# Leftover keys scored and applied in eight single pieces in the middle of each attention sweep

## The reference, cut to what matters

```python
x = x + jnp.tanh(g_xattn[3]) * _L3_xattn_ref(...)      # q, k, v projections, then per head:
# scores = q @ k.T * 8 ** -0.5 ; p = softmax(scores, axis=-1) ; out = (p @ v) @ Wo + bo
x = x + jnp.tanh(g_ffn[3]) * _L3_ffn_ref(_layernorm(x, axis=-1), ...)
```

## Time and profile before

| | us |
|---|---|
| median of 3 runs | 3082.24 (3079.79 to 3084.54) |
| the profiled execution, its time | 3080.51 |
| its span on the core | 3078.7 |
| TensorE (PE) busy | 3009.3, 98% |
| ScalarE (ACT) busy | 2519.7, 82% |
| VectorE (DVE) busy | 467.2, 15% |
| exponentials of the sweeps, x2496 | 2283.0 |
| value products (line 2343) | 1324.3 |
| score products (line 2362) | 1064.4 |
| chain that ended last | PE 94% |

### The profile page before, as it was taken

How to read it: one execution, slowest core, us unless ns; L and a number is a source line. 1 busy time by engine, 2 the same in 40 slices (tenths; PEclk the granted TensorE clock), 3 DMA queues, 4 the chain that set the end, 5 groups by cost and what they waited for, 6 DMA issues and landing times.

```text
span 3078.7 us, 54520 instructions
## 1 busy us (share of the span) xinstructions
PE 3009.3 (98%) x18701; PEld 1140.2 (37%) x18701; DVE 467.2 (15%) x1308; ACT 2519.7 (82%) x2893; POOL 206.1 (7%) x732
## 2 busy tenths in 40 slices
PE   7999999999999899999999998999999999999999
PEld 5333333323334433333323334666522222332257
DVE  4200001001011400111101004544200000000012
ACT  3899999999933499999999995322499999999963
POOL 4000000000000000000000002000000000000000
PEclk9999999999999999999999999999999999999999
DMA  7122122112220112122211223110011111111110
GB/s 198 54 63 64 58 63 68 38 37 63 63 75 0 29 58 69 54 63 65 64 38 39 63 63 112 32 37 1 8 38 37 37 37 54 47 38 36 37 38 8
DMA packets 167028, 157.27 MB, mean 51 GB/s; under 512 B 20872, under 2 KB 121724, under 8 KB 166844
## 3 DMA queue, kind: packets, MB, share of 16 engines
q1 hardware_dynamic: 159872, 149.27, 16.1%
q0 software_dynamic: 1088, 3.34, 0.3%
q10 hardware_dynamic: 5884, 2.08, 0.3%
HBM read 121.89 MB, written 32.91 MB: 50 GB/s over the span
## 4 chain that ended last, share of the span: by engine, by line
PE 94%; DVE 3%; DMA 1%; issue 1%; ACT 1%; SPq 1%; ACTq 0%; DVEq 0%
PE PS L2343 40%; PE PS L2362 31%; PE PS L774 5%; PE PS L759 5%; PE PS L761 2%; PE PS L1114 2%; PE PS L1104 1%; PE PS L1572 1%; PE PS L1569 1%; PE PS L1148 0%; PE PS L1105 0%; PE PS L2323 0%; PE PS L2253 0%; PE PS L2329 0%; PE PS L1134 0%
## 5 line engine op out<-in xcount | busy, mean ns | idle before, releaser
L2110 ACT ACTIVATE probs<-PS 128x1024 f32<-128x1024 f32 x2496 | 2283.0, 1227 | 37.8 <-PE PS L2362 32.9
L2343 PE MATMUL PS<-probs,vr 128*32 128x512 f32 (+1 forms) x9984 | 1324.3, 603 | 1.9 <-DVE accs L2590 1.9
L2362 PE MATMUL PS<-qs,kr 35*128 35x512 f32 (+2 forms) x4992 | 1064.4, 481 | 8.7 <-ACT probs L2110 3.3
L2362 PEld LDWEIGHTS PS<-qs,kr 35*128 35x128 f32 x4992 | 448.0, 184 | 1181.9 <-ACT probs L2110 816.0
L797 ACT ACTIVATE probs<-PS 128x512 f32<-128x512 f32 x192 | 114.5, 598 | 273.6 <-PE PS L759 145.5
L1939 POOL COPY vr<-vs 128x72 f32 (+1 forms) x624 | 157.8, 253 | 2668.9 <-PE PS L2343 2466.5
L2343 PEld LDWEIGHTS PS<-probs,vr 128*32 128x32 f32 x9984 | 197.2, 108 | 339.2 <-issue 272.1
L774 PEld LDWEIGHTS PS<-wide,probs 128*128 128x128 f32 x1280 | 152.7, 195 | 17.5 <-issue 16.5
L774 PE MATMUL PS<-wide,probs 128*128 128x128 f32 x1280 | 155.1, 279 | 0.5 <-DVE kf L832 0.5
L2590 DVE COPY accs<-PS 128x512 f32<-128x512 f32 x12 | 8.3, 692 | 750.1 <-PE PS L2329 750.1
L759 PE MATMUL PS<-xT,wide 128*128 128x512 f32 x224 | 106.7, 594 | 1.0 <-DVE probs L816 1.0
(11 more groups left out here) (315 smaller groups left out, 1185.8 us busy)
## 6 DMA issues: line engine op xcount, KB each, us to landing
kr<-key_pieces SPq DMA_DIRECT2D x1248, 64.0 KB
key_pieces<-kparts SPq DMA_DIRECT2D x172, 96.0 KB, 2.8
kr<-mask_strips SPq DMA_DIRECT2D x624, 4.0 KB
values<-kf SPq DMA_DIRECT2D x34, 216.0 KB, 4.2
vs<-values SPq DMA_DIRECT2D x2, 3672.0 KB, 16.1
c_T<-turned_context SPq DMA_DIRECT2D x18, 192.0 KB, 4.0
key_pieces<-probs SPq DMA_DIRECT2D x32, 96.0 KB, 2.9
c_in<-turned_context SPq DMA_DIRECT2D x16, 192.0 KB, 4.3
```

The source lines that it names most:

```text
L2110: sc.activation(prob[n % RING][:, :, q0:], PS[:, bank:bank + 2, q0:], ACT.Exp, scale=SCALE).then_inc(p_ready, 1)
L2343: last = te.matmul(PS[32 * j:32 * j + 32, 7, q0:], vr[s.buf(c)][:, at_v:at_v + 32], prob[(n + j // 2) % RING][:, j % 2, q0:], start=fresh, ...
L2362: last = te.matmul(o, kr[b][own, p, :], qs[own, T8 // 2 * s.hh + p, 512 * s.qh + q0:512 * s.qh + 512], start=True, stop=True)
```

## The change

The leftover keys are now handled inside the sweep that they belong to. Round 9 (`LEFT_ROUND`) takes the four score products one at a time and round 10 takes the value product in four pieces of 128 columns. Each piece stands behind a value group, in four neighbouring half chunks: behind (c, g) = (0, 1), (1, 0), (1, 1) and (2, 0). The exponential stands in ScalarE's list between rounds 9 and 10. The seams and the ends of the attentions have only the last value groups left. VectorE's copy of the accumulator waits for the last value group (`pv_done`) as well. The items of round 9 are moved to the third chunk of round 10, those of round 10 to the first of round 11, those of round 11 behind them. The loops of sweeps 8, 9 and 11 on TensorE are cut in two, with six chunks written out between them.

```diff
@@ ScalarE
                         for p in range(4):
                             exps(c, p)
-                            if prev and (c, p) == (0, 1):
-                                exps_left(prev)
                     with act.Fori(1, EXP_ROUND) as i:
...
                                 exps(c, p, i)
+                    exps_left(s)
...
-                    if s.w % NSW == NSW - 1:
-                        exps_left(s)
@@ TensorE
+                def left_free(s):
                     if s.w % NSW == 0:
                         pe.wait_ge(left_in, LEFT_IN * (a + 1))
                     if s.w:
                         pe.wait_ge(left_done, s.w)
+                    if s.w % NSW == 2:
+                        if a == 0:
+                            pe.wait_ge(early_ev, EARLY_AT[0] + 3)
+                        else:
+                            pe.wait_ge(r_cen, (0, 1, 3)[a])
+                    own = [(w, i) for w in range(s.w + 1) for i in range(1, ROUNDS_S) if w < s.w or i < LEFT_ROUND]
+                    pe.wait_ge(v_ev, NTILE + sum(len(later_items(w, i)) for w, i in own))
+                def left_score(s, tt):
+                    if tt == 0:
+                        left_free(s)
+                    t8 = T8 // 2 * s.hh + tt
+                    last = te.matmul(PS[:, 6, :], k_left[:, P * t8:P * t8 + P], qs[:, t8, 512 * s.qh:512 * s.qh + 512], start=(tt == 0), stop=(tt == T8 // 2 - 1),
+                                     skip_group_check=True)
+                    if tt == T8 // 2 - 1:
+                        last.then_inc(left_ready, 1)
+                def left_value(s, k):
+                    if k == 0:
+                        pe.wait_ge(left_done, s.w + 1)
+                    last = te.matmul(PS[:, 7, k * P:k * P + P], v_left[:, s.hh, :], p_left[:, k * P:k * P + P], start=False, stop=True, skip_group_check=True)
+                    if k == 3:
+                        last.then_inc(left_used, 1)
+                def left_slot(s, i, c, g):
+                    slot = 2 * c + g - 1
+                    if i == LEFT_ROUND and 0 <= slot < 4:
+                        left_score(s, slot)
+                    if i == LEFT_ROUND + 1 and 0 <= slot < 4:
+                        left_value(s, slot)
...
                         values(prev, prev.n - 1, 0)
-                        left_scores(prev)
                     scores(0, 1)
                     if prev:
                         values(prev, prev.n - 1, 1)
-                        left_values(prev)
...
                             items = later_items(s.w, i)
+                            if i == LEFT_ROUND:
+                                items = []
+                            if i == LEFT_ROUND + 1:
+                                items = [None] * (TC - 1) + later_items(s.w, LEFT_ROUND)
+                            if i == LEFT_ROUND + 2:
+                                items = later_items(s.w, i - 1) + items
...
                                     values(s, i * TC + c - 1, g)
+                                    left_slot(s, i, c, g)
...
-                        with pe.Fori(1, ROUNDS_S) as i:
+                        with pe.Fori(1, LEFT_ROUND) as i:
...
+                        for c in range(LEFT_ROUND * TC, (LEFT_ROUND + 2) * TC):
+                            for g in range(2):
+                                scores(c, g)
+                                values(s, c - 1, g)
+                                left_slot(s, c // TC, c % TC, g)
+                        with pe.Fori(LEFT_ROUND + 2, ROUNDS_S) as i:
@@ VectorE
                     dve.wait_ge(left_used, s.w + 1)
+                    dve.wait_ge(pv_done, s.quads + 2 * s.n)
```

More of the change, by code:

```diff
@@ L57 @@
 EXP_ROUND = 10
+LEFT_ROUND = EXP_ROUND - 1
 NSW = 4
@@ L1171, in early_dve @@
                 dve.wait_ge(left_ready, 2)
+                dve.wait_ge(pv_done, SWEEPS[2].quads)
                 leaf_turn_dve(dve, 0, 6).then_inc(early_ev, 1)
@@ L1784, in _ @@
                                 sp.wait_ge(left_ready, s.w)
+                                sp.wait_ge(pv_done, s.quads)
                             if 2 * TC <= c < 2 * TC + 6 and a == 0:
@@ L2312, in _ @@
                 pe.wait_ge(qc_dve, QU // 2 * (a + 1))
-                def left_scores(s):
+                def left_free(s):
                     if s.w % NSW == 0:
@@ L2319, in left_scores @@
                         pe.wait_ge(left_done, s.w)
-                    pe.wait_ge(v_ev, NTILE + sum(len(later_items(w, i)) for w in range(s.w + 1) for i in range(1, ROUNDS_S)))
-                    for tt in range(T8 // 2):
-                        t8 = T8 // 2 * s.hh + tt
-                        last = te.matmul(PS[:, 6, :], k_left[:, P * t8:P * t8 + P], qs[:, t8, 512 * s.qh:512 * s.qh + 512], start=(tt == 0), stop=(tt == T8 // 2 - 1))
-                    last.then_inc(left_ready, 1)
-                def left_values(s):
-                    pe.wait_ge(left_done, s.w + 1)
-                    te.matmul(PS[:, 7, :], v_left[:, s.hh, :], p_left[:, :], start=False, stop=True, skip_group_check=True).then_inc(left_used, 1)
+                    if s.w % NSW == 2:
[25 more added lines that the diff above has]
+                        left_value(s, slot)
                 def values(s, c, g, i=0):
@@ L2383, in _ @@
                                     values(s, i * TC + c - 1, g)
-                                if c < len(items):
+                                    left_slot(s, i, c, g)
+                                if c < len(items) and items[c]:
                                     later_pe(pe, *items[c])
@@ L2388, in _ @@
                     else:
-                        with pe.Fori(1, ROUNDS_S) as i:
+                        with pe.Fori(1, LEFT_ROUND) as i:
+                            for c in range(TC):
+                                for g in range(2):
+                                    scores(c, g, i)
+                                    values(s, c - 1, g, i)
+                        for c in range(LEFT_ROUND * TC, (LEFT_ROUND + 2) * TC):
+                            for g in range(2):
+                                scores(c, g)
+                                values(s, c - 1, g)
+                                left_slot(s, c // TC, c % TC, g)
+                        with pe.Fori(LEFT_ROUND + 2, ROUNDS_S) as i:
                             for c in range(TC):
@@ L2398, in _ @@
                     if s.w % NSW == NSW - 1:
-                        left_scores(s)
                         for g in range(2):
                             values(s, s.n - 1, g)
-                        left_values(s)
                 between_pe(pe, a)
```

## The result

| | before | after |
|---|---|---|
| median | 3081.01 (3078.21 to 3084.54, 4 runs) | 3136.65 (3121.90 to 3150.18, 4 runs) |
| ratio, 95% interval | | 1.0172 [1.0145, 1.0198] |
| the profiled execution, its time | 3080.51 | 3150.18 |
| its span | 3078.7 | 3148.4 |

A later comparison of the same two kernels gave 3134.93 us and 1.0181 [1.0143, 1.0219] (the last experiment). The forecast was 3104.0 us, 3088 to 3111. The direction was right and the size was not: of 55.6 us, it had 22.5. Executions of one kernel differ by up to 28 us here (3121.90 to 3150.18), and the profiled one of after is its slowest; the fastest had a mean granted clock of TensorE of 0.984, the slowest of 0.973.

The account below looks back on a forecast made before the run. ScalarE sets the pace, TensorE waiting 0.17 us a half chunk. Gains of 11.9 us against costs of 34.4 give net 22.5 us more: 3103.0 from the profiled execution, 3104.7 from its median; forecast 3104.0 us, range 3088 to 3111.

Parts of the forecast that it names:

- part 5: First sweep of each attention: the first score piece waits for operand loads; 15.0 us lost, 13.5 to 19.2.
- estimate of 12.6 us: Loss from the three operand waits by the skill page's fixed DMA cost of about 2.0 us: 12.6 us.
- The slack of 0.17 us a half: Steady half chunk: it repeats every 1.83 us, TensorE needs 1.66, so its lag shrinks by 0.17 us.
- Rival C: At the operand waits: loads land in time or the wait is met earlier; 15.0 us go, 3090 us; chance 0.09.
- Rival E: Late key loads, loop switching beyond the cushion, or operands landing at 4.2 us: 3109 to 3112 us; chance 0.06.
- B: Rounds 9 and 10: pieces are seamless and cost their columns alone; net +5.4 us, 3088 us; chance 0.08.
- D: Mid sweep: the cushion is deeper, up to 2.75 us, so pieces lose nothing; +1.1 us, 3083 us; chance 0.05.
- part 3: Rounds 9 and 10: lone pieces take 0.43 and 0.41 us, losing 1.26 us a sweep, 15.1 us; exponentials 1.5 us.
- part 4: Items moved behind the pieces in six sweeps: 2.6 us lost, and 0.2 us for transposes in sweep 2.
- parts 1 and 2: Leftover work gone from the seams gains 6.0 and 0.5 us, from the three attention ends 5.4 us.
- what would show it wrong: Halves with a piece last no longer than those without, or the first piece starts unwaited in the first sweeps.
- the cushion: TensorE's lead over ScalarE: inserted work is hidden up to 0.54 us, everything above is ScalarE's loss.

Follow-up runs that it names:

- the last experiment: The changed kernel run once more, unchanged, against the kernel before: 3134.93 us, ratio 1.0181.
- the filled wait: The changed kernel with 25, 25 and 18 unused products ahead of the operand wait in sweeps 0, 4 and 8: 3116.63 us, ratio 1.0119.
- the first experiment: The changed kernel with two small v_left loads per chunk instead of one, all landed long before round 9: 3093.19 us, ratio 1.0033.
- The two lumps: The first experiment with four score products together in round 9 and the value product whole in round 10: 3088.91 us, ratio 1.0027.
- The waits without pieces: The changed kernel without the leftover keys' products and exponentials, but with the operand wait in sweeps 0, 4 and 8: 3099.37 us, ratio 1.0058.

## Why the prediction was wrong

**The step that failed is part 5, the price of the wait.** It said that all of the wait is ScalarE's loss, and stopped there: 15.0 us, 19.2 at most. Its length was nearly right: 5.84, 6.20 and 4.62 us of standstill against 5.65, 5.56 and 3.83, because the load let TensorE go 3.07, 3.51 and 3.66 us after its issue and not after 2.8 (2374.82 - 2371.16 in sweep 8). The prediction's estimate of 12.6 us was further off: the Trainium skill, DMA: Bandwidth & Descriptors, Anatomy of one DMA, gives its fixed cost of about 2.0 us for the path of GpSimd, and this load is SyncE's. What was missing is that TensorE's speed depends on TensorE not standing still. The slack of 0.17 us a half, by which the whole sum is made, exists at 2.4 GHz only; at 1.2 GHz TensorE needs 3.01 us for a half that ScalarE needs 1.83 for, and each such half loses 1.18 us, or 3.74 - 1.83 = 1.91 with a piece. Over 20 to 34 us of low clock this comes to 29.2 us for the three in the first trace and 23.7 in the second, against 17.0 for the length of the waits. The sum had this term at nothing. Put into it: 3104.7 + 1.6 for the longer waits + 29.2 is 3135.5, and with 23.7 it is 3130.0; the medians were 3136.65 and 3134.93. That the first of the two comes so near is partly luck, since its 29.2 is from the slowest execution.

The profile of before could have warned me. It has stretches of low clock in the opening of sweep 0 (10.2 us from 99.7) and between the attentions, and I read the clock only where I wanted to know the pace. The Trainium skill, TensorE: Matmul & The Clock Gate, HAM oscillation — how this bites in real kernels, tells of a kernel whose waits for DMAs let the clock fall each time. The traces agree: it fell behind each of the fourteen unfilled waits of 2.27 us and more. I did not weigh it. It prices the fall as half of the throttled time. By that, as an estimate, the 75.1 us of low clock at the three places in the first trace would be 37.5; the comparison with the filled wait gives 29.2, since part of the low clock lies in the standstill and in what ScalarE's own pace covers.

**Rival C was the kernel one edit away.** It had 3090 for no wait; the early loads gave 3093.19. Its mechanism, that the loads land in time, was wrong for the changed kernel and its price was good. Rival E named later operands and gave 3109 to 3112; it had the right side and the wrong mechanism. B and D fell: the pieces are neither seamless nor hidden.

**Right, the pieces (part 3).** In sweep 9, which no wait disturbs:

```profile
2568.11 0.49 PE L2333 MATMUL PS<-qs,k_left 128*128 128x512 f32 x1
...
2570.20 0.49 PE L2333 MATMUL PS<-qs,k_left 128*128 128x512 f32 x1
...
2576.45 0.73 PE L2385 MATMUL PS<-qs,kr 35*128 35x512 f32 x4
2577.11 1.06 PE L2366 MATMUL PS<-probs,vr 128*32 128x512 f32 x8
2578.11 0.49 PE L2385 MATMUL PS<-qs,kr 35*128 35x512 f32 x2
...
2580.29 0.49 PE L2342 MATMUL PS<-p_left,v_left 128*128 128x128 f32 x2
...
2582.37 0.49 PE L2342 MATMUL PS<-p_left,v_left 128*128 128x128 f32 x2
```

A half with a score piece takes 2.09 us and one with a value piece 2.08, against 2578.11 - 2576.45 = 1.66: 0.43 and 0.42 us a piece, where 0.43 and 0.41 were forecast. A value piece has a quarter of a score piece's columns, in two passes, and costs as much; about half of each is the fixed part. The two lumps take 1.13 + 1.05 us of TensorE in place of 4 x 0.43 + 4 x 0.42 = 3.4, and the 1.2 us saved are six times 0.2. With the Trainium skill's rule, TensorEngine Tiling (Array Packing), Key Properties, that a change of tiling mode drains TensorE, the runs agree; they show the price of a product that stands alone, and not that the drain is what it pays for. Rival B's price, the columns alone, would have made the pieces free to ScalarE, and they were not. ScalarE lost 1.22 to 1.30 us a sweep in sweeps 1, 3, 5, 7, 8, 9 and 11 of the first experiment; 1.26 was the forecast.

**Right, the items (part 4).** From before to the first experiment, rounds 9 to 11 lose 17.8 us more over the twelve sweeps. Parts 3 and 4 have 15.1 + 2.6 + 0.2 = 17.9.

**Right, the seams and the ends (parts 1 and 2).** ScalarE runs through the seam from sweep 8 to 9, where the earlier trace rows have an idle time of 0.72 us, and in the second attention the next work starts close behind the last exponential:

```profile
2464.15 13.57 ACT L2113 ACTIVATE probs<-PS 128x1024 f32<-128x1024 f32 x14
```

```profile
1936.50 0.71 ACT L2113 ACTIVATE probs<-PS 128x256 f32<-128x256 f32 x2 [0.31 <-DVE PS L2624]
```

```profile
1937.26 0.43 PE L2366 MATMUL PS<-probs,vr 128*32 128x128 f32 x8 [0.23 <-ACT probs L2113]
1937.62 3.70 PE L760 MATMUL PS<-h_T,wide 128*128 128x512 f32 x8
```

From the last exponential's end, 1937.21, to the next product there are 0.41 us; before there were 1881.57 - 1879.13 = 2.44. That is the 2.0 us forecast. In the first and the third attention the same stretch shrinks from about 2.7 to 1.05 us, where 1.7 us were forecast each. One seam was mis-sized: from sweep 6 to 7 before loses 1.31 us, and 0.5 without the leftover where the clock stays up, so 0.8 us are gained there and not 0.17.

**Of what would show it wrong**, I had named pieces that take no time and a missing wait; the pieces took their time and the wait was there. I named no sign in the granted clock, the one column that would have shown the error.

## What stays open

How long the clock stays low varies, from 6.8 to 47.8 us at places that look alike, with TensorE fully busy. No run here says what decides it, nor why it falls at some emptied seams behind 0.3 to 1.2 us of idle time and not behind 0.74 to 1.06 us at the three places. The waits without pieces cost 26.7 us by their medians. The waits with pieces cost 43.5. A half with a piece loses 0.73 us more at the low clock than one without. In the first trace of after 15 pieces fell into low clock (7, 4 and 4), which gives 11 us of the 16.8 between the two, if nothing is taken off for what the same pieces cost at full clock. Whether the pieces also make the low clock last longer is not settled: the profiled execution without pieces had it low for as long as the two with them, but it was one of the three slowest of ten. That the clock falls less in some executions is on record with their mean granted clocks: the fastest run without pieces, 3087.56 us, which is what the length of the waits alone would give, had 0.987, and the three slowest, 3106.49 to 3108.10 us, had 0.979 and 0.980. The kernel before spreads in the same way, from 3072.99 us at 0.993 to 3093.50 at 0.986, so a gain of 5 us is not read from single executions.

## What to carry to other kernels

Price a new wait of TensorE twice: its length, and what the work behind it costs at half the clock, for some 20 us (6.8 to 47.8 here), if TensorE is nearly the bound there. The second can be the larger. Loading the operand a few microseconds earlier takes both away, and idle products ahead of the wait take away the second (in the profiled execution wholly, by the medians for the most part). Before small products are moved from a seam to the middle of a paced stretch, work out the cushion and what is won back in each step: pieces further apart than their cost divided by that slack are free, pieces closer are not.

## What the runs showed of the chip that I had not expected

- A standstill of TensorE of 2.27 us was enough for its granted clock to fall to 1.2 GHz for 47.8 us; 0.74 to 1.06 us at the three places did not do it. But length alone does not decide: in emptied seams of the second attention it fell, for 3.4 to 20.5 us, where TensorE's longest idle time was 0.3 to 1.2 us.
- Once it had fallen behind one of the waits, the clock stayed low for 20 us and more in eleven of fourteen cases, with TensorE busy after the wait (the other three: 6.8, 6.8 and 10.2 us).
- A small load behind two key loads and a strip load let TensorE go 3.07 to 3.66 us after its issue, later than the key stores' 2.8 us on the same queue.
